# A selective scan with five constant products a chunk added on TensorE, and 16-row products padded to 128 rows

## The reference

```
def _mamba_fwd(hidden_states, ...):                      # 512 inner features, 16 states
    xz = einsum('bld,ed->ble', hidden_states, in_proj_w)
    x, z = split(xz, 2, axis=-1)
    u = silu(conv(transpose(x)) + conv1d_b)              # 4 taps along the sequence
    x_dbl = einsum('bld,rd->blr', ut, x_proj_w)          # 48 columns:
    dt_low, B_var, C_var = x_dbl[:16], x_dbl[16:32], x_dbl[32:48]
    delta = softplus(einsum('blr,dr->bld', dt_low, dt_proj_w) + dt_proj_b)
    dA = exp(delta[..., None] * A)
    dBu = delta[..., None] * B_var * ut[..., None]
    h = dA * h + dBu ; y = einsum('bdn,bn->bd', h, C)    # step by step along the sequence
    return einsum('bld,ed->ble', (y + ut * D_param) * silu(z), out_proj_w)
x = layernorm(x + mamba(x))                              # "x1" below
x = layernorm(x + experts(x))
```

## Time and profile before

| | |
|---|---|
| median of three runs | 4417.06 us |
| profiled execution | 4411.45 us |
| its span | 4409.7 us |
| TensorE matmul busy | 82% of the span |
| VectorE busy | 86% |
| ScalarE busy | 78% |
| GpSimd busy | 79% |

### The profile page before, as it was taken

One profiled execution on the slowest core, in us unless ns is written; L12 is line 12 of the kernel. 1 busy time (PEld: TensorE's weight loads), 2 busy tenths in 40 slices (PEclk: granted clock), 3 DMA queues, 4 the chain that ended last, 5 costly groups with the idle time before them and its releaser, 6 DMA issues. The chain is left out here.

```text
span 4409.7 us, 57988 instructions
## 1 busy us (share of the span) xinstructions
PE 3621.9 (82%) x19574; PEld 2535.3 (57%) x19574; DVE 3809.4 (86%) x4906; ACT 3450.5 (78%) x5856; POOL 3471.0 (79%) x1757
## 2 busy tenths in 40 slices
PE   8788888888888888888888888888865499999990
PEld 3455555555555555555555555555554388888880
DVE  5999999999999999999999999999995665665545
ACT  6888988898888888888888988888871265565656
POOL 3889989999899999999989999999882255555533
PEclk9899999999999999999999999999976699999995
DMA  2566666666666666666666666666652133333328
GB/s 85 137 153 163 155 152 154 162 154 157 153 150 157 152 153 162 156 157 152 167 146 158 149 153 154 152 158 154 153 133 48 59 73 64 61 62 64 64 30 309
DMA packets 179621, 592.74 MB, mean 134 GB/s; under 512 B 33392, under 2 KB 99056, under 8 KB 128128
## 3 DMA queue, kind: packets, MB, share of 16 engines
q0 software_dynamic: 70080, 332.96, 39.1%
q1 hardware_dynamic: 104640, 239.32, 15.7%
q10 hardware_dynamic: 4608, 16.78, 0.9%
HBM read 221.47 MB, written 68.68 MB: 66 GB/s over the span
## 5 line engine op out<-in xcount | busy, mean ns | idle before, releaser
L436 POOL TENSOR_TENSOR dbu<-du,bb 128x2048 f32<-128x2048 f32 x511 | 2397.1, 4726 | 202.7 <-DVE h L849 178.8
L849 DVE TENSOR_TENSOR_SCAN h<-da,hlast,dbu 128x512 f32<-128x512 f32 x1536 | 1873.7, 1264 | 27.6 <-POOL dbu L436 20.8
L492 ACT ACTIVATE da<-dl,negA 128x512 f32<-128x512 f32 x2048 | 1397.3, 693 | 216.6 <-DVE h L849 214.0
L742 PE MATMUL ht<-ident,h 128*128 128x128 f32 x8192 | 1216.8, 297 | 349.0 <-ACT pair L511 178.6
L742 PEld LDWEIGHTS ht<-ident,h 128*128 128x128 f32 x8192 | 1014.7, 153 | 761.3 <-DVE h L849 320.0
L849 DVE TENSOR_TENSOR_SCAN h<-da,dbu 128x512 f32<-128x512 f32 x512 | 593.5, 1203 | 11.6 <-ACT da L492 7.4
L511 ACT ACTIVATE pair<-ht,ct 128x512 f32<-128x512 f32 x768 | 512.0, 681 | 86.7 <-PE ht L742 84.3
L666 PE MATMUL spare<-xin,win 128*128 128x512 f32 x1024 | 491.8, 610 | 9.1 <-DMA xin<-in_xt 7.5
L675 PE MATMUL spare<-xh,conv 128*128 128x512 f32 x1024 | 463.4, 595 | 0.8 <-ACT xh L523 0.8
L857 DVE SCALAR_TENSOR_TENSOR pair<-ht,ct,pair 128x512 f32<-128x512 f32 x544 | 393.4, 728 | 50.7 <-PE ht L742 50.6
L1410 ACT ACTIVATE hraw<-f,b 128x512 f32<-128x512 f32 x256 | 176.3, 689 | 260.8 <-PE f L1468 244.9
(11 more groups left out here) (183 smaller groups left out, 5576.6 us busy)
## 6 DMA issues: line engine op xcount, KB each, us to landing
acc<-pair POOLq DMA_DIRECT2D x190, 1024.0 KB, 7.3
bb<-b_rows SPq DMA_DIRECT2D x128, 1024.0 KB, 5.1
acc<-acc POOLq DMA_DIRECT2D x64, 1024.0 KB, 8.6
dl<-du POOLq DMA_DIRECT2D x62, 512.0 KB, 7.7
xin<-in_xt SPq DMA_DIRECT2D x32, 512.0 KB, 8.4
xres<-in_x SPq DMA_DIRECT2D x32, 512.0 KB, 8.7
x_scores<-xres SPq DMA_DIRECT2D x32, 512.0 KB, 3.0
sums<-xres SPq DMA_DIRECT2D x32, 512.0 KB, 4.0
```

What stands on the lines that cost most here:

```text
L436: pool.tensor_tensor(dbu[n % 2][:], du[q][:], bb[part % 2][:, m:m + 1, :].to_broadcast([P, DT, CH]), ALU.mult).then_inc(dbu_done, 1)
L492: act.activation(da[DA_SLOT[m]][:], dl[q][:, dt, :], ACT.Exp, scale=negA[:, dt, n:n + 1]).then_inc(exp_done, 1)
L742: last = te.transpose(ht[HT_SLOT[m]][:, dt * P:(dt + 1) * P], h[n % 2][:, dt, b * P:(b + 1) * P], ident[:])
L849: dve.tensor_tensor_scan(h[n % 2][:, dt, :], da[DA_SLOT[n * DT + dt]][:], dbu[n % 2][:, dt, :], start, ALU.mult, ALU.add).then_inc(scan_do ...
```

## The change

Three things are changed, all in `stage1`. First, the D products run over 128 rows in place of 16: `wdt` and `xdbl` become tiles of 128 partitions, GpSimd clears both at the start, SyncE waits for that before it loads the small weights, and the x-projection is still copied into the first 48 partitions. Second, a table `FILL` puts products of constant tiles (the first diagonal matrix times 512 columns of `wo`) ahead of two steps: three ahead of T0 and two ahead of D0. They write the same buffer as the step that follows, which overwrites them. Third, for that they stand behind the wait on `prev` and ahead of the step's own wait.

```diff
+FILL = {("T", 0): 3, ("D", 0): 2}
...
-        wdt = a.sb("wdt", [16, 512])
+        wdt = a.sb("wdt", [P, 512])
+        wdt_rows = wdt[0:16]
...
-        xdbl = a.sb("xdbl", [48, CH])
+        xdbl = a.sb("xdbl", [P, CH])
...
                 load_xin(0, 0)
+                sp.wait_ge(padded, 1)
...
+                pool.memset(wdt[:], 0.0).then_inc(padded, 1)
+                pool.memset(xdbl[:], 0.0).then_inc(padded, 1)
                 pool.memset(ident[:], 0.0).then_inc(ident_ok, 1)
...
-                        act.copy(xdbl[:], bank[0:48, :]).then_inc(done, 1)
+                        act.copy(xdbl[0:48, :], bank[0:48, :]).then_inc(done, 1)
...
                     if prev:
                         s, v = step_done(*prev)
                         te.wait_ge(s, v)
                     f, p = c + 1, c - 1
                     done = pe[GROUP[kind]]
+                    if not is_first(f):
+                        for _ in range(FILL.get((kind, i), 0)):
+                            te.matmul(bank[:], conv[:, 0, 0, :], wo[:, 0:2, :], start=True, stop=True)
...
-                        last = te.matmul(bank[:], wdt[:, i * P:(i + 1) * P], xdbl[0:16, :],
+                        last = te.matmul(bank[:], wdt[:, i * P:(i + 1) * P], xdbl[:],
                                          start=True, stop=True)
```

More of the change, by code:

```diff
@@ L223, in stage1 @@
         relu_ok, last_summed = S("first_relu_ready"), S("last_pairs_added")
+        padded = S("rows_padded")
         set_ok, negA_ok, conv_ok = S("constants_set"), S("negA_ready"), S("conv_ready")
@@ L331, in _ @@
                 load_xin(0, 0)
+                sp.wait_ge(padded, 1)
                 for dst, src in ((wconv, d["wconv"]), (vecs, d["vecs"]), (wx, d["wx"]), (negA, d["alog"]),
-                                 (wdt, d["wdt"]), (wo, d["wo"]), (gate, d["gate"])):
+                                 (wdt_rows, d["wdt"]), (wo, d["wo"]), (gate, d["gate"])):
                     sp.dma_start(dst[:], src).then_inc(loaded, 16)
@@ L535, in evacuate @@
                     elif kind == "XP":
-                        if not is_first(f):
+                        if is_first(f):
+                            act.wait_ge(padded, 2)
+                        else:
                             act.wait_ge(b_out, 16 * f)
-                        act.copy(xdbl[:], bank[0:48, :]).then_inc(done, 1)
+                        act.copy(xdbl[0:48, :], bank[0:48, :]).then_inc(done, 1)
                     elif kind == "CT":
@@ L686, in step @@
                         for b in range(NB):
-                            last = te.transpose(bank[:, b * 48:b * 48 + 48], xdbl[:, b * P:(b + 1) * P],
+                            last = te.transpose(bank[:, b * 48:b * 48 + 48], xdbl[0:48, b * P:(b + 1) * P],
                                                 ident[0:48, 0:48])
```

## The result

| | before | changed |
|---|---|---|
| median | 4416.27 us (4413.94 to 4420.0, 4 runs) | 4455.0 us (4452.46 to 4464.13, 4 runs) |
| profiled execution, span | 4411.45, 4409.7 us | 4452.46, 4450.7 us |
| ratio | 1 | 1.0091, 95% interval 1.0073 to 1.0108 |

The change makes the kernel 39 us slower. I had forecast 18 us slower, 4435, with 4402 to 4476 as the range: the direction and the mechanisms hold, the size is off by more than a factor of two.

The account below looks back on a forecast made before the run. VectorE's work plus its waits was taken to bound the kernel. 54 us lost at T0 less 36 won at D0 gave +18 on 4417, so 4435 us, with a range of 4402 to 4476.

Parts of the forecast that it names:

- What bounds the kernel: Stage 1: a chunk costs VectorE's work plus its waits; a microsecond of wait is about a microsecond of kernel.
- D: At D0 to D2: wider rows cost 0, two added products fit in cover, full clock wins 36 of 50.6 us.
- T0, the mechanism: Products start when T0 began, not in an x1 wait; VectorE waits at (5, 0), 0.8 us full clock, 4.2 half.
- T0, the share: At T0: half the chunks at 0.8 us, half at 2.8, mean 1.8; 54 us over 30 chunks.
- The first: Added products keep the clock full at T0, which then costs only 24 us: faster, 4400 us; chance 0.2.
- The second: T0's mean wait of 0.9 to 1.5 us meets the 36 us won: 4408 to 4426 us; chance 0.2.
- The fourth: The gain at D0 does not come, T0's 54 us stand alone: 4471 us; chance 0.1.
- The third: T0's products meet half clock in nearly all chunks, 3.5 us in 30: +69 us, 4486 us; chance 0.1.

Follow-up runs that it names:

- the D part alone: Changed kernel without the three products ahead of T0; 128-row D and two products ahead of D0 stay: 4374.47 us, ratio 0.9904 to the kernel before.
- the run with Y3: Changed kernel with two more added products ahead of Y3, not for the last chunk: 4403.94 us, ratio 0.997 to the kernel before.

## Why the prediction was right or wrong

**What bounds the kernel: right.** A microsecond of VectorE's wait was a microsecond of the kernel: +40.0 us of wait and +39 us in the medians; -39.2 and -42 for the D part alone.

**D: right.** 36 us were booked, 39.2 is what the waits show. D's rows took no more time (the pair of D0 1.02 us), the added pair of products fitted into its cover, and ScalarE took D0 3.0 us after TensorE had come to this place, against 3.2 in the kernel before. The three quarters of the 50.6 us that were put at this place, 38, are 39.4 in the trace. What the text left open is which half does it: for this wait either does most of it, in time the rows 35 us and the products 21.

**T0, the mechanism: right.** There was no wait for x1; the products began when T0 had begun; block (5, 0) waited. The prices at either clock were right too: 0.8 forecast and 0.78 to 0.90 measured at full clock, 4.2 as the upper bound and 3.56 to 3.91 with the products at half clock throughout, less because the clock comes back during T0 or the first turn.

**T0, the share: wrong, and this is the failed step.** "I take half of the chunks at full clock (0.8) and half in a half-clock stretch that ends on the way (2.8)" gave 1.8 us. Measured are 6 of 29 chunks at full clock and 23 at a mean of 3.05 (11 at 2.37 with part of the products at half clock, 12 at 3.67 with all of them), 2.59 together: 30 x 2.6 = 78 us in place of 54. The share alone, at the forecast prices, turns the 54 into 72; the price of the slow chunks (3.05 for 2.8) does the rest. With 78 the sum would have been 4417 + 78 - 36 = 4459, against 4455 measured. Half and half came from two chunks that I had looked at, one of each kind. The trace of the kernel before had the answer, had I asked for all chunks. Six in a row of it, 2.6 us from the start of T0 on (length, TensorE busy, PEclk, DMA):

```profile
503.84:506.44 2.60, 2.60 (x14) 0.59 1.00 202
605.38:607.98 2.60, 2.41 (x16) 0.76 1.10 224
709.65:712.25 2.60, 2.60 (x12) 0.50 1.06 214
812.33:814.93 2.60, 2.60 (x12) 0.50 1.12 227
913.44:916.04 2.60, 2.60 (x14) 0.59 1.00 202
1014.82:1017.42 2.60, 1.97 (x16) 1.00 1.09 221
```

Five of the six have half clock in it, and 24 of the 29 chunks from 2 to 30. Some of these stretches begin just after T0's start (the 0.59 and 0.76), where they hardly touch T0, but do touch three products put in its place. And the argument that dense products would end such a stretch sooner was too hopeful: in 12 of 29 chunks all three ran through at half clock. The row of the added products in the changed kernel says the same in one number:

```profile
L671 PE MATMUL spare<-wo,conv 128*128 128x512 f32 x316 | 200.7, 779 | 56.5 <-DVE g L880 55.7 <-DVE xres L886 0.8
```

A row of 512 columns has 592 ns at full clock; 779 is the mean over all 316, although those ahead of D0 ran at full clock in all 29 chunks. These counts are of one execution. The four runs of the changed kernel are 12 us apart, so the share may differ from one to the next.

**The rivals.** The first (clock full at T0) did not come by itself; the run with Y3 made it come, and got 4404 us where the rival had 4400. The second (a draw) needed a mean wait of 0.9 to 1.5 us; it was 2.59. The fourth (no gain at D0) is excluded by the D part alone. The third (3.5 us in each of 30 chunks, 4486) overshot: 12 of 29 had that.

**The chances.** Slower had 0.6. The main uncertainty was one number, the share, and that could have been counted.

## What to carry to other kernels

A product that is to fill a wait must stand in it: behind the wait for its own output buffer it fills nothing, and pushes back all that stands behind it, which is free only as far as the next readers come late enough, as at D0. For each engine that reads what comes later, compare the added time at half clock with the distance to its next read. Where a cost depends on the clock, count the state over all repetitions of the place, not over the two that were looked at, and remember that an addition is exposed to more of the time line than what stood there before.

## What the runs showed of the hardware

D products over 16 and over 128 rows take about the same time at full clock (pairs of 1.12 and 1.02 us at D0, 1.98 us for D1 and D2 with either), but they do not leave the same clock. With nothing changed but the rows, VectorE's wait for turned blocks went from 50.6 to 19.0 us, and TensorE stood at the 2.4 GHz level for more of stage 1. The stretch from 200 to 3200 us, in the kernel before (length, TensorE busy, PEclk, DMA) and in the one with the rows alone (all engines):

```profile
200.00:3200.00 3000.00, 2523.88 (x12077) 0.93 0.65 155
```
```profile
200.00:3200.00 3000.00, 2456.21 (x12161) 1614.71 (x12160) 2937.31 (x3256) 2676.74 (x4584) 2758.99 (x1183) 0.96 0.65 156
```

The mean clock is 0.96 against 0.93, and TensorE is busy 68 us less although it gets through somewhat more of the program. Over whole executions the granted clock was 0.927 to 0.929 in the five runs with the rows and 0.901 to 0.911 in the fifteen of the kernel before beside them. What is done at one place of a chunk also changed how often the half clock met another: with the same three products ahead of T0, 12 of 29 chunks had all of them at half clock in the kernel with the D part and 7 of 29 in the one without, each counted in one execution.
